# Two batches begin the rotary layers beside the last two batches' experts

## Chip, cores and metric

One core of a Trainium2 chip runs the whole program. The metric is the device time in microseconds (us); the three timed runs of the kernel before gave 4245.79, 4249.10 and 4255.25 us, so their median is 4249.1 us. Engine names are those of the profile: PE (TensorE), DVE (VectorE), ACT (ScalarE), POOL (GpSimd), SP (SyncE, whose queue issues all transfers).

## What is computed

The input x has 4 batches of 512 tokens with 128 features. The reference adds eight blocks in turn, each on a layer norm of x:

```python
x = x + L0_xcond(...)   # 3 rounds of slot attention against 77 context rows      -> stage 0
x = x + L0_ffn(...)     # 8 experts, top 2 of the 7 farthest, by similarity       -> stage 1
x = x + L1_xcond(...)   # 16 heads of 64, keys: 512 tokens and 77 context rows    -> stage 2
x = x + L1_ffn(...)     # 8 experts, the best one                                 -> stage 3
x = x + L2_xcond(...)   # self attention, cross attention, gated feed forward     -> stage 4
x = x + L2_ffn(...)     # 16 experts of width 64 in 4 groups, and shared ones     -> stage 5
x = x + L3_xcond(...)   # 6 layers, 16 heads of 8 with rotary positions           -> stage 6
x = x + L3_ffn(...)     # feed forward on the better half of the tokens           -> stage 7
```

One of the 6 rotary layers is: normalise, scale and shift; queries and keys projected and rotated by position; softmax(q k / sqrt 8) v over 512 tokens with a mask; the same again against the 77 context rows; a feed forward layer of width 512. Stages 6 and 7 are planned together, so "stage 6" below means both.

## The kernel before

**How the order comes about.** The kernel is a planner and five engine programs. Each piece of work is a Python generator that yields a `Want`: a chain of engines with estimated costs, and the buffers that it takes. `Plan.merge` always takes the Want whose key is smallest (the estimated time at which its first engine can begin, terms for work done and for the kind of chain, and a seeded random term), advances the planner's clocks and lets the generator emit its steps. The resulting list is the order of the instructions on every engine; each engine then runs strictly in its own order and waits on semaphores. The constants of the key are set for each stage in `ORDER`.

**Streams.** In stage 0 four streams run, one for each batch. After it, `fence("0")` closes the list of stage 0 and the clocks are levelled. Then two chains run (c.i is 0 and 1); chain 0 takes batches 0 and 2, chain 1 batches 1 and 3, through stages 1 to 5. In the expert stages 1, 3 and 5 `ahead` lets the gates of the second batch be computed beside the experts of the first. When both chains are through stage 4, the weights of rotary layers 0 and 1 are loaded into the two slots `WL` of the area wA (`lay0`), and `init6` is spawned: POOL fills the query and key areas of the four batches (memsets, L2706 and L2710) and SP then writes the mask rows into them (L1386 to L1391). When both chains are through stage 5, `bar` makes PE, ACT, DVE and POOL wait for each other, `mk6` (DVE) writes the mask columns of the value tiles, and the four streams `stage6` begin with `context6`, which projects the context's keys and values for each layer.

**A rotary layer** (`layer`): `ln6` (statistics L2156 and L2160 on DVE, the power on POOL, the normalisation L2169 on DVE or L2717 on POOL, transposes L1779, ACT L2061); `rope` twice, for keys and queries: PE projects (L1788, four matmuls in two banks), DVE multiplies by cosine and sine (L2538), POOL adds the halves and splits the sum into three bf16 parts (L2723 to L2736), and SP copies the parts to the tiles KS and QS (L1400). The value projection is L1796. Then `attn6`. Its softmax subtracts an exact row maximum, so `maxima` comes ahead of the scores: for self attention 32 reductions in each batch (`m8`: two matmuls at L1815, one reduction at L2549), for cross attention 8 (`m8c`: L1827, L2556). After each half of them `m8t` splits the maxima into a high and a low bf16 part (DVE L2562, L2564), PE transposes them (L1837), ACT copies the result (L2081), and SP writes it (`md`, L1405) into two rows of the query tile. Then `s8` makes the scores (L1847), ACT the exponential (L2088), and `a8` multiplies by the values (L1861).

**Tiles that matter here.** In stage 5 the second batch of a chain keeps its small tiles at columns 4096 to 4904 of its area `ar`, where the value tile V8 of batches 0 and 1 lies in stage 6. The experts' step in stage 5 is L1750 (two projections, four matmuls), L1756 (the weight spread over the rows), DVE L2506 and L2511, and L1764 (back to 128 features); DVE L2516 and L2518 add the result to X. In stages 0 and 1 the lines are L2249 (DVE, result of stage 0 to X), L1469 and L1538 (transposes and gates) and L1572 and L1580 (experts).

## Time and profile before

| what | value |
|---|---|
| median of three runs | 4249.1 us |
| the profiled execution, own time | 4243.65 us |
| its span, first to last instruction | 4241.9 us |
| mean granted TensorE clock | 0.956 |
| PE busy | 3750.9 us (88%) |
| DVE busy | 2500.4 us (59%) |
| ACT busy | 2365.3 us (56%) |
| POOL busy | 1356.9 us (32%) |

Busy shares are means over the span, and the stages have different limits: the tables by stretch say what an engine did in one stage. In a row of the timeline, the number in square brackets is the time the engine stood idle before the instruction, and what ended it. A granted clock of 1.00 is 2.4 GHz and 0.50 is 1.2 GHz.

### The profile page before, as it was taken

What the parts mean: (1) busy time and instruction counts of PE and PEld (TensorE: products, weight loads), DVE (VectorE), ACT (ScalarE), POOL (GpSimd) and SP (SyncE); (2) the same over time, 40 slices, a digit from 0 to 9 for tenths busy, and PEclk for the clock granted to TensorE, in tenths of its full rate; (3) what the DMA queues carried; (4) which work ended last, traced back from release to release, by engine and by line L of the source; (5) the groups of instructions that cost most, each with busy time, mean ns of one, the idle gap of its engine ahead of it and who ended that gap; (6) DMA issues with size and microseconds to landing.
All of it is one profiled execution on the core that took longest, in us unless ns stands there. A gap on an engine that the chain in (4) does not pass through costs nothing.

```text
span 4241.9 us, 58462 instructions
## 1 busy us (share of the span) xinstructions
PE 3750.9 (88%) x23161; PEld 1690.0 (40%) x23161; DVE 2500.4 (59%) x4892; ACT 2365.3 (56%) x3312; POOL 1356.9 (32%) x1333
## 2 busy tenths in 40 slices
PE   5599999899999998998886789988899898898996
PEld 3377433333774334334453123333333333332333
DVE  6731444544224444543566977787777777777754
ACT  4543554454335545555421477676676777767783
POOL 5500233334003430351033133434434343342412
PEclk8699999999999999999987899999999999999997
DMA  2000100000000001001101110210201101111100
GB/s 96 20 1 1 40 16 21 11 11 21 26 1 34 17 26 37 6 21 45 31 28 43 27 32 24 59 29 24 64 24 36 52 27 44 42 39 31 40 12 16
DMA packets 103826, 124.73 MB, mean 29 GB/s; under 512 B 25059, under 2 KB 88747, under 8 KB 101624
## 3 DMA queue, kind: packets, MB, share of 16 engines
q1 hardware_dynamic: 103552, 120.99, 9.5%
q8 instruction: 182, 2.98, 0.3%
q14 instruction: 92, 0.75, 0.1%
HBM read 58.00 MB, written 1.45 MB: 14 GB/s over the span
## 4 chain that ended last, share of the span: by engine, by line
PE 60%; DVE 23%; ACT 7%; POOL 6%; issue 2%; DMA 1%; SPq 0%; POOLq 0%; DVEq 0%; ACTq 0%
PE ps L1676 6%; PE ps L1660 6%; PE ps L1580 6%; PE ps L1572 5%; PE ps L1861 5%; DVE c1sm L2549 4%; DVE c0sm L2549 4%; PE ps L1788 3%; PE ps L1847 2%; PE ps L1708 2%; PE ps L1601 2%; PE ps L1815 2%; ACT wB L2088 2%; PE ps L1905 2%; POOL c1m L2717 2%
## 5 line engine op out<-in xcount | busy, mean ns | idle before, releaser
L2088 ACT ACTIVATE wB<-ps 128x1024 f32<-128x1024 f32 (+1 forms) x771 | 771.9, 1022 | 252.3 <-PE ps L1847 244.8
L2549 DVE TENSOR_REDUCE c1sm<-ps 128x2 f32<-128x1024 f32 x384 | 454.2, 1218 | 107.5 <-PE ps L1815 105.2
L2549 DVE TENSOR_REDUCE c0sm<-ps 128x2 f32<-128x1024 f32 x384 | 452.0, 1218 | 95.7 <-PE ps L1815 94.3
L2386 DVE TENSOR_REDUCE c1sm<-ps 128x2 f32<-128x1024 f32 x128 | 151.2, 1218 | 182.5 <-PE ps L1625 181.8
L2386 DVE TENSOR_REDUCE c0sm<-ps 128x2 f32<-128x1024 f32 x128 | 151.9, 1219 | 174.8 <-PE ps L1625 174.3
L2088 ACT ACTIVATE c0m<-ps 128x1024 f32<-128x1024 f32 (+1 forms) x189 | 193.2, 1022 | 59.0 <-PE ps L1847 57.4
L1861 PE MATMUL ps<-wB,c1m 128*9 128x512 f32 (+1 forms) x1224 | 202.2, 601 | 0.2 <-ACT wB L2088 0.2
L1660 PE MATMUL ps<-c0ar 64*128 64x512 f32 (+1 forms) x640 | 176.8, 629 | 13.6 <-DVE c1sm L2386 5.9
L1847 PE MATMUL ps<-c0ar 64*128 64x512 bf16 (+1 forms) x864 | 164.5, 386 | 26.8 <-DVE c1sm L2549 8.2
L2656 POOL TENSOR_SCALAR c0ve<-c0mv 128x4 f32<-128x4 f32 x25 | 6.2, 249 | 561.5 <-DVE c0mv L2160 550.3
L1660 PE MATMUL ps<-c1ar 64*128 64x512 f32 (+1 forms) x640 | 178.5, 634 | 8.0 <-ACT c1ar L2015 4.6
L1847 PE MATMUL ps<-c1ar 64*128 64x512 bf16 (+1 forms) x864 | 165.1, 390 | 21.9 <-DVE c0sm L2549 7.2
L2656 POOL TENSOR_SCALAR c0sm<-c0sm 128x4 f32<-128x4 f32 x40 | 7.8, 195 | 531.9 <-DVE c0sm L2160 453.5
L2700 POOL TENSOR_TENSOR c0ar<-c0ar 128x1024 f32<-128x1024 f32 x52 | 123.5, 2374 | 170.0 <-ACT c0ar L2022 137.3
L1815 PE MATMUL ps<-c0ar 62*128 62x512 bf16 x768 | 152.3, 397 | 25.1 <-DVE c0sm L2549 12.1
L2723 POOL TENSOR_TENSOR c0m<-c0m 128x512 f32<-128x512 f32 (+1 forms) x78 | 96.1, 1234 | 239.7 <-DVE c0m L2538 217.8
L2022 ACT ACTIVATE c1ar<-ps 128x1024 f32<-128x1024 f32 (+1 forms) x97 | 99.3, 1024 | 128.0 <-PE ps L1663 126.8
L1815 PE MATMUL ps<-c1ar 62*128 62x512 bf16 x768 | 151.5, 395 | 21.2 <-DVE c1sm L2549 7.4
L2656 POOL TENSOR_SCALAR c1sm<-c1sm 128x4 f32<-128x4 f32 x40 | 7.8, 195 | 500.4 <-DVE c1sm L2160 499.4
L2022 ACT ACTIVATE c0ar<-ps 128x1024 f32<-128x1024 f32 (+1 forms) x96 | 98.3, 1024 | 115.3 <-PE ps L1663 113.3
L2700 POOL TENSOR_TENSOR c1ar<-c1ar 128x1024 f32<-128x1024 f32 x53 | 126.1, 2379 | 113.1 <-ACT c1ar L2022 84.8
L1580 PEld LDWEIGHTS ps<-wA,c0m 128*128 128x128 f32 x1024 | 134.1, 193 | 56.9 <-issue 56.4
(841 smaller groups left out, 8609.2 us busy)
## 6 DMA issues: line engine op xcount, KB each, us to landing
c0ar<-c0m SPq DMA_DIRECT2D x216, 128.0 KB, 2.4
c1ar<-c0m SPq DMA_DIRECT2D x216, 128.0 KB, 2.4
c0m<-rscr SPq DMA_DIRECT2D x96, 128.0 KB, 2.9
c1m<-rscr SPq DMA_DIRECT2D x96, 128.0 KB, 2.9
wA<-in_lay SPq DMA_DIRECT2D x6, 1346.0 KB, 5.8
wA<-in_w SPq DMA_DIRECT2D x1, 4248.0 KB, 21.9
wA<-in_w SPq DMA_DIRECT2D x1, 4104.0 KB, 13.7
wA<-in_w4b SPq DMA_DIRECT2D x1, 2948.0 KB, 9.6
```

What stands on the lines that cost most here:

```text
L1572: e.matmul(u.ap, w1, z, start=True, stop=True).then_inc(*T(("ex1", n), free=[zt] if zt else []))
L1580: i = e.matmul(j4(acc.ap, j), j4(h.ap, j), w2, start=(k == 0 and j == 0), stop=(k == 3), skip_group_check=True)
L1660: e.matmul(j4(u.ap, h, 512)[0:n, :], c.KT[s][r, o:o + n], c.QT[s][r, :], start=True, stop=False)
L1676: x = e.matmul(acc.ap[64 - 64 * h:128 - 64 * h, :], c.VV[g % 2][0:n, i, 64 * h:64 * h + 64], P.ap[0:n, h, :], start=first, stop=end, skip_ ...
L1815: i = e.matmul(j4(u.ap, p, 512), c.QS[r, s, 128 * j:128 * j + 128], c.KS[r, s, :], start=True, stop=True)
L1847: i = e.matmul(j4(u.ap, p, 512)[0:n, :], K, c.QS[r, s, :], start=True, stop=True)
L1861: x = e.matmul(acc.ap[32 * i:32 * i + (9 if g % 2 else 18), :], vv, Ps[i // 2].ap[0:n, i % 2, :], start=first, stop=end, skip_group_check= ...
L2022: e.activation(P.ap[0:n, :, :], u.ap[0:n, :].rearrange("p (h q) -> p h q", h=2), ACT.Exp, scale=0.125).then_inc(*A(("P", n0, g, i), free=[u]))
L2088: e.activation(P.ap[0:n, :, :], u.ap[0:n, :].rearrange("p (a q) -> p a q", a=2), ACT.Exp, scale=S8).then_inc(*A(("P8", n0, s, k), free=[u]))
L2386: e.tensor_reduce(c.sm[:, 2 * (g % 2), 2 * j:2 * j + 2], u.ap.rearrange("p (h k) -> p h k", h=2)[:, :, 0:n], AX, ALU.max, negate=True).the ...
L2549: e.tensor_reduce(c.mneg[:, s // 4, j, :, s % 4], u.ap.rearrange("p (a k) -> p a k", a=2), AX, ALU.max, negate=True).then_inc(*V(free=[u]))
L2700: e.tensor_tensor(S.ap, P0.ap if P0 else S.ap, P.ap, ALU.add).then_inc(*G(("S", n0, g), free=[P0, P] if P0 else [P]))
```

## The change

Three things are done, and the planner's constants of stages 5 and 6 are set anew (stage 5: `held` 0.05 to 0.0066, `table` 2.0 to 2.1037, `spread` 1.0 to 1.0158, seed 2625 to 1721, three of the biases; stage 6 in the diff).

- **Stage 0 is joined to stage 1.** Instead of two merges with a fence and levelled clocks between them, one merge runs from the start to the end. A chain begins stage 1 when its own first batch is through stage 0; its second batch's gates wait until that batch is through (`zero`). When all four batches and the adaptive scales are through, fence 0, the load of w2 and `init64` are emitted (`through`), and the constants of stage 1 come in. The steps of stage 0 are planned by the same constants and seed as before.
- **Batches 0 and 1 begin stage 6 early.** After the experts of its first batch a chain spawns `begin6`. It waits in the planner for the last step of `init6`, marks all engines (`fence(("h", i))`), lets DVE wait for those marks (`hs`), and runs `stage6` for that batch: layer norm, projections, rotation and all 32 reductions. Values, the transposed maxima and the scores come only when `opened` is set, behind the bar of stage 5. Until then the two batches work in the slot of layer 1's weights (`E6` for the transposed activations, and `ER`, one buffer of 1280 columns, for the normalised activations and for every rotation of both batches), and their running sum `y` lies behind that slot. So layer 1's weights are loaded later, by `lay1`, whose transfer waits on SP for the early rotations and the two value projections. Batches 2 and 3 and `context6` begin behind the bar.
- **Cross attention's maxima are turned once.** `m8w` and `mw` treat all eight slices together (one split on DVE, four transposes of 32 rows on PE, one copy on ACT, two transfers) where `m8t` and `md` ran twice. Self attention keeps two halves. The tiles mneg and MS are laid out for both.

```diff
--- before.py
+++ after.py
...
-    "6": dict(lag=0.0689, weight=0.0152, even=0.002, held=0.2395, table=1.1712, apart=56.5442, spread=0, seed=9094, stagger=13.3148, bias=dict(T=0.244, S=0.373, VTA=-0.191, TVb=-0.054, A=-0.534, VG=-0.949, G=-0.490, TA=-0.046, TAb=-0.043)),
+    "6": dict(lag=0.0241, weight=0.0152, even=0.002, held=0.2549, table=1.1712, apart=56.5442, spread=0, seed=3843, stagger=13.3148, bias=dict(T=0.244, S=0.373, VTA=-0.191, TVb=-0.054, A=-0.534, VG=-0.949, G=-1.010, TA=-0.046, TAb=-0.043)),
...
-            e.mneg = s[:, 64:128].rearrange("p (h j a s) -> p h j a s", h=2, j=4, a=2)
-            e.MS = s[:, 128:192].bitcast(BF).rearrange("p (h j r) -> p h j r", h=2, j=4)
+            e.mneg = s[:, 64:128].rearrange("p (j a h s) -> p j a h s", j=4, a=2, h=2)
+            e.MS = s[:, 128:192].bitcast(BF).rearrange("p (j h r) -> p h j r", j=4, h=2)
+            e.MW = s[:, 128:192].bitcast(BF).rearrange("p (j r) -> p j r", j=4)
...
-            e.y = carve(512).rearrange("p (t d) -> p t d", t=4)
+            e.y = wA[:, 2 * LCOLS + 512 * e.i:2 * LCOLS + 512 * e.i + 512] if e.i < 2 else carve(512)
+            e.y = e.y.rearrange("p (t d) -> p t d", t=4)
...
+        E6 = Bufs([wA[:, LCOLS + 512 * k:LCOLS + 512 * k + 512] for k in range(2)])
+        ER = Bufs([wA[:, LCOLS + 1024:LCOLS + 2304]])
...
-        def ahead(gates, rest, c):
+        def ahead(gates, rest, c, then=None):
 
             q, got = c.alt, []
             q.ring = c.ring
 
             def second():
+                while 2 + c.i not in zero:
+                    yield
                 got.append((yield from gates(q, 2 + c.i, 0.0)))
 
             g = yield from gates(c, c.i, 0.0)
             plan.spawn(second(), c)
             yield from rest(c, c.i, *g)
+            if then:
+                plan.spawn(then(c), six[c.i])
             while not got:
                 yield
             yield from rest(q, 2 + c.i, *got[0])
 
-        begun, done, quarter = {}, {}, []
+        begun, done, quarter, zero, opened = {}, {}, [], set(), []
+
+        def through(what):
+
+            zero.add(what)
+            if len(zero) == 5:
+                fence("0")
+                emit("load", "w2", "wB", "0")
+                plan.stage("1")
+                for c in cos:
+                    plan.spawn(init64(c), c)
+
+        def scales():
+            yield from adaptive()
+            through("ada")
+
+        def opening(c):
+
+            yield from stage0(c, c.i)
+            through(c.i)
+            if c.i < 2:
+                while "en" not in first:
+                    yield
+                c.work = ORDER["0"]["stagger"] + ORDER["1"]["apart"] * c.i
+                yield from chain(c)
 
         def chain(c):
 
             for name, run in (("1", lambda: ahead(stage1, experts1, c)), ("2", lambda: both(stage2, c)),
                               ("3", lambda: ahead(stage3, experts3, c)), ("4", lambda: both(stage4, c)),
-                              ("5", lambda: ahead(stage5, experts5, c))):
+                              ("5", lambda: ahead(stage5, experts5, c, begin6))):
+                while name == "2" and len(zero) < 5:
+                    yield
                 if name in "24":
                     pairs_of_ring(c)
                 elif name in "35":
                     ring_of_pairs(c)
                 if name not in begun:
                     begun[name] = c
-                    plan.stage(name)
+                    if name != "1":
+                        plan.stage(name)
                     emit("gate", {"1": ("w_w1", "w1"), "2": ("w_w2", "w2"), "3": ("w_w3", "w3"), "4": ("w_w4a", "w4a"),
                                   "5": ("w_w5", "w5")}[name])
                 yield from run()
                         emit("load", "w4b", "wA", "3")
                         emit("sel")
                     elif name == "4":
-                        for l in range(2):
-                            emit("lay0", l)
+                        emit("lay0", 0)
                         plan.spawn(init6())
+                    elif name == "5":
+                        emit("bar", "5")
+                        plan.level(banks)
+                        emit("mk6")
+                        plan.stage("6", six)
+                        opened.append(True)
+                        for e in six[2:]:
+                            plan.spawn(stage6(e), e)
+                        plan.spawn(context6())
+
+        def begin6(c):
+
+            e = six[c.i]
+            e.work = c.work
+            while "i6" not in first:
+                yield
+            fence(("h", c.i))
+            emit("hs", c.i)
+            yield from stage6(e)
...
+            first["i6"] = True
...
             def maxima():
-                for h in range(2):
+                if cross:
+                    for s in range(8):
+                        (u,), t = yield Want([("T", .27), ("V", .73)], [two], tq, True)
+                        emit("m8c", c, l, n0, s, qn, kkeys, u)
+                        two.give(u, t[1])
+                    (u,), t = yield Want([("V", .5), ("T", .35), ("A", .6)], [banks], t[1])
+                    emit("m8w", c, n0, u)
+                    banks.give(u, t[2])
+                    _, t = yield Want([("S", 1.3)], after=t[2])
+                    emit("mw", c, n0)
+                    got[0] = got[1] = t[0]
+                    return
+                def half(h):
+                    t = (0.0, tq)
                     for s in range(4 * h, 4 * h + 4):
-                        if cross:
-                            (u,), t = yield Want([("T", .27), ("V", .73)], [two], tq, True)
-                            emit("m8c", c, l, n0, s, qn, kkeys, u)
+                        for j in range(4):
+                            (u,), t = yield Want([("T", .32), ("V", 1.24)], [two], tq, True)
+                            emit("m8", c, n0, s, j, qn, kkeys, u)
                             two.give(u, t[1])
-                        else:
-                            for j in range(4):
-                                (u,), t = yield Want([("T", .32), ("V", 1.24)], [two], tq, True)
-                                emit("m8", c, n0, s, j, qn, kkeys, u)
-                                two.give(u, t[1])
-                    (u,), t = yield Want([("V", .42), ("T", .35), ("A", .6)], [banks], t[1])
+                    return t[1]
+
+                def turned(h, t):
+                    (u,), t = yield Want([("V", .42), ("T", .35), ("A", .6)], [banks], t)
                     emit("m8t", c, n0, h, u)
                     banks.give(u, t[2])
                     _, t = yield Want([("S", 1.3)], after=t[2])
                     emit("md", c, n0, h)
                     got[h] = t[0]
+
+                if opened:
+                    for h in range(2):
+                        t = yield from half(h)
+                        yield from turned(h, t)
+                    return
+                for h in range(2):
+                    t = yield from half(h)
+                while not opened:
+                    yield
+                for h in range(2):
+                    yield from turned(h, t)
 
...
-        lay_ready = {0: True, 1: True}
+        lay_ready = {0: True}
+        early = []
         lay_done = {}
         kc = {}
         cross_done = {}
             b = c.i
             w = WL[l % 2]
             s, sh = ada(3 + 3 * l, b)
-            zt, key, t = yield from ln6(c, c.t, s, sh, "G" if l else "V")
+            begins = l == 0 and b < 2
+            zb, ztb, rb = (ER, E6, ER) if begins else (G6, G6, R6)
+            zt, key, t = yield from ln6(c, c.t, s, sh, "G" if l else "V", zb, ztb)
             got = {}
 
             def keys():
-                got["k"] = yield from rope(f"k{b}", w["k"], zt.ap, key, 512, c.KS, KR, [c.ks_free], t)
+                got["k"] = yield from rope(f"k{b}", w["k"], zt.ap, key, 512, c.KS, KR, [c.ks_free], t, rb)
 
             def queries():
-                got["q"] = yield from rope(f"q{b}", w["q"], zt.ap, key, 512, c.QS, QR, [c.qs_free], t)
+                got["q"] = yield from rope(f"q{b}", w["q"], zt.ap, key, 512, c.QS, QR, [c.qs_free], t, rb)
+
+            n = uid()
+
+            def values():
+                while not opened:
+                    yield
+                (u,), tv = yield Want([("T", 1.1), ("A", 1.15)], [banks], t)
+                emit("v8", c, n, w["v"], zt, key, u, c.vf)
+                banks.give(u, tv[1])
+                got["v"] = tv[1]
+
+            def over():
+                while len(got) < 3:
+                    yield
+                emit("endz", zt)
+                ztb.give(zt, max(got["v"], t))
+                if begins:
+                    early.append((b, got["k"][0], got["q"][0], n))
+                    if len(early) == 2:
+                        yield from do("lay1", list(early), chain=[("S", .7)], after=got["v"])
+                        lay_ready[1] = plan.clock["S"] + 30.0
 
             plan.spawn(keys(), c)
             plan.spawn(queries(), c)
-            n = uid()
-            (u,), tv = yield Want([("T", 1.1), ("A", 1.15)], [banks], t)
-            emit("v8", c, n, w["v"], zt, key, u, c.vf)
-            banks.give(u, tv[1])
+            plan.spawn(values(), c)
+            plan.spawn(over(), c)
...
-        plan.stage("0", four)
-        plan.merge([context(), constants()] + [stage0(c, c.i) for c in four] + [adaptive(), norms()], [None, None] + four)
-        fence("0")
-        plan.level(banks)
-        emit("load", "w2", "wB", "0")
-        for c in cos:
-            c.work = ORDER["1"]["apart"] * c.i
-        plan.merge([chain(c) for c in cos] + [init64(c) for c in cos], cos)
-        emit("bar", "5")
-        plan.level(banks)
-        emit("mk6")
-        plan.stage("6", six)
-        plan.merge([stage6(c) for c in six] + [context6()], six)
+        plan.stage("0")
+        for c in four:
+            c.work = ORDER["0"]["apart"] * (c.i // 2)
+        plan.merge([context(), constants()] + [opening(c) for c in four] + [scales(), norms()], [None, None] + four)
         fence("6")
...
+            def lay1(uses):
+                for b, kn, qn, vn in uses:
+                    w.wait_ge(*D(f"k{b}").at(("rp", kn)))
+                    w.wait_ge(*D(f"q{b}").at(("rp", qn)))
+                    w.wait_ge(*T.at(("v8", vn)))
+                e.dma_start(wA[:, LCOLS:2 * LCOLS], d["lay"][1]).then_inc(*D("w_l1")(("lay", 1)))
...
+            def mw(c, n0):
+                w.wait_ge(*A.at(("mT", n0)))
+                for p in range(2):
+                    e.dma_start(c.QS[64 * p + 62:64 * p + 64, :, :], c.mT[16 * p:16 * p + 16, :]
+                                ).then_inc(*D(f"m{c.i}_0")(("m", n0, 0)))
...
+            def hs(i):
+                for q in (T, A, V, G):
+                    w.wait_ge(*q.at(("f", ("h", i))))
...
+            def m8w(c, n0, u):
+                MW = c.MW.rearrange("p j (a x h s) -> p (j a) x (h s)", a=2, x=2, h=2)
+                hi, lo, m = MW[:, :, 0, :], MW[:, :, 1, :], c.mneg.rearrange("p j a h s -> p (j a) (h s)")
+                w.wait_ge(*V.now())
+                e.tensor_copy(hi, m).then_inc(*V())
+                w.wait_ge(*V.now())
+                e.tensor_tensor(lo, m, hi, ALU.subtract).then_inc(*V(("ms", n0)))
+                mss[c.i, 0] = mss[c.i, 1] = V.n
```

## Rows read from the trace of the kernel before

**Rows 1.** The page, chain of waits that ended last, by engine.

```profile
PE 60%; DVE 23%; ACT 7%; POOL 6%; issue 2%; DMA 1%; SPq 0%; POOLq 0%; DVEq 0%; ACTq 0%
```

**Rows 2.** By stretch: PE, PEld, DVE, ACT, POOL busy (count), PE clock, DMA share, GB/s.

```profile
190.00:210.00 20.00, 2.97 (x12) 2.49 (x12) 13.13 (x59) 3.73 (x7) 5.75 (x12) 0.50 0.29 106
2190.00:2212.00 22.00, 20.24 (x94) 12.61 (x92) 14.33 (x49) 3.44 (x5) 0.67 (x1) 1.00 0.03 8
2212.00:2263.50 51.50, 50.27 (x214) 30.93 (x214) 22.44 (x33) 9.54 (x14) 0.00 (x0) 0.97 0.00 1
2263.50:2320.00 56.50, 28.64 (x86) 17.01 (x86) 37.93 (x120) 8.05 (x23) 29.35 (x40) 0.67 0.22 57
2320.00:2377.00 57.00, 28.56 (x98) 5.87 (x97) 56.67 (x53) 0.00 (x0) 15.40 (x16) 0.58 0.16 43
2390.00:4050.00 1660.00, 1489.22 (x10983) 534.97 (x10981) 1285.83 (x1993) 1187.50 (x1400) 620.93 (x739) 0.99 0.13 37
...
2900.00:3000.00 100.00, 85.97 (x652) 29.15 (x650) 77.98 (x116) 69.20 (x81) 34.49 (x40) 0.98 0.15 42
```

**Rows 3.** Timeline of DVE about the end of stage 5.

```profile
2145.32 0.69 DVE L2516 TENSOR_TENSOR X<-X,ps 128x512 f32<-128x512 f32 x1
...
2230.90 0.69 DVE L2516 TENSOR_TENSOR X<-X,ps 128x512 f32<-128x512 f32 x1 [2.33 <-PE ps L1770]
...
2262.75 0.69 DVE L2516 TENSOR_TENSOR X<-X,ps 128x512 f32<-128x512 f32 x1 [2.33 <-PE ps L1770]
...
2266.82 0.87 DVE L2156 BATCH_NORM_STATS2 c0sm<-X 128x6 f32<-128x128 f32 x4
...
2358.22 18.18 DVE L2549 TENSOR_REDUCE c0sm<-ps 128x2 f32<-128x1024 f32 x16
2376.43 0.18 DVE L2562 CAST c0sm<-c0sm 128x32 bf16<-128x32 f32 x1
```

**Rows 4.** Timeline of PE about the same place.

```profile
2257.74 1.88 PE L1750 MATMUL ps<-c1ar,wB 128*128 128x512 f32 x4
...
2285.70 1.88 PE L1788 MATMUL ps<-c1m,wA 128*128 128x512 f32 x4
...
2371.93 0.61 PE L1815 MATMUL ps<-c0ar 62*128 62x512 bf16 x2 [0.52 <-DVE c0sm L2549]
...
2382.34 0.39 PE L1815 MATMUL ps<-c0ar 62*128 62x512 bf16 x2
2382.57 0.38 PE L1847 MATMUL ps<-c0ar 64*128 64x512 bf16 x2
```

**Rows 5.** Timeline of POOL: memsets of init6, and one rotation's first and last step.

```profile
2137.96 7.11 POOL L2706 MEMSET c0ar<- 128x4096 bf16 x2
...
2188.52 2.15 POOL L2710 MEMSET c1ar<- 128x2464 bf16 x1
...
2334.62 1.26 POOL L2723 TENSOR_TENSOR c0m<-c0m 128x512 f32<-128x512 f32 x1 [2.54 <-DVE c0m L2538]
...
2338.54 1.15 POOL L2736 TENSOR_TENSOR c0m<-c0m 128x512 bf16<-128x512 f32 x1
```

**Rows 6.** Timeline of SP's queue: the first transfers of turned maxima.

```profile
2378.14 1.42 SPq L1405 DMA_DIRECT2D c0ar<-c0m  x2
```

**Rows 7.** Timeline of DVE: the same four normalisations beside a memset and without one.

```profile
2137.85 7.36 DVE L2169 TENSOR_SCALAR c1m<-X,c1mv,c1rs 128x128 f32<-128x128 f32 x4 [0.77 <-POOL c1rs L2658]
...
2377.64 1.11 DVE L2169 TENSOR_SCALAR c1m<-c1m,c1sm 128x128 f32<-128x128 f32 x4
```

**Rows 8.** Waits between 2390 and 4050: engine, line, whom; us in total, times, longest.

```profile
PE ps L1837 <- DVE c0sm L2564: 27.9, 42, 1.4
PE ps L1837 <- DVE c1sm L2564: 24.1, 36, 2.3
```

**Rows 9.** Timeline of PE: one batch's turn; stage 1's first expert matmuls.

```profile
2907.11 0.39 PE L1837 MATMUL ps<-IDB,c0sm 128*16 128x128 bf16 x4 [0.61 <-DVE c0sm L2564]
...
215.96 4.86 PE L1572 MATMUL ps<-c0m,wA 128*128 128x512 f32 x6
```

**Rows 10.** Timeline of DVE: the last result of stage 0 goes to X.

```profile
194.90 0.69 DVE L2249 TENSOR_TENSOR X<-X,c1ar 128x512 f32<-128x512 f32 x1
```

72 lines of the change are left out of this document (43 added, 29 removed).

## Prediction, made before the changed kernel ran

> **What bounds the kernel now.** I read the chain of waits first: 60% of it is PE and 23% DVE [rows 1], so most of the time is worth what PE's time is worth, and a quarter of it is a DVE story. The busy time by stretch shows where. In the body of stage 6 PE is busy 1489.22 of 1660 us, 89.7%, beside DVE's 77.5% and ACT's 71.5% [rows 2]. The last 51.5 us of stage 5 are PE alone (50.27 us, DVE 22.44, POOL nothing) [rows 2]. Between them lies a hole: from 2263.5 to 2377 PE is busy 57.2 of 113.5 us at a granted clock of 0.67 and 0.58, and in its second half DVE is busy 56.67 of 57 us [rows 2]. The DVE timeline names the work: layer norms from 2266.82, then back to back reductions until 2376.43 [rows 3]; the PE timeline shows each pair of maxima matmuls waiting 0.52 us for the reduction before it, and the first score matmul at 2382.57 [rows 4]. Batch 0 had its result of stage 5 at 2145.32 and batch 1 at 2230.90; the last batch came at 2262.75 [rows 3]. A smaller hole lies between stages 0 and 1: in 190 to 210 PE is busy 2.97 of 20 us at 0.50 [rows 2].
>
> **Part 1, early batches.** When can they begin? Batch 0 is done at 2145.32 but must wait for the memsets, which end at 2190.67 [rows 5]. From the first layer norm to the end of the second projection took 20.8 us (2266.82 to 2287.58) [rows 3, 4]; a rotation takes POOL 5.1 us (2334.62 to 2339.69) [rows 5]. Keys and queries now share one buffer ER, so the second rotation waits for the first's transfers; I put 40 us from the start to the first reduction, against about 54 us before with four batches mixed (2266.82 to 2320, from where DVE does nothing but reduce) [rows 2, 3]. So batch 0 reduces from about 2230 and batch 1 from about 2275.
>
> What it adds to stage 5: PE gets two rotations' projections of 1.88 us each per batch and 32 pairs of 0.39 us [rows 4]: 3.8 + 12.5, with transposes some 17 us for batch 0 and 5 for what batch 1 reaches. PE is full there, so this is paid: stage 5 ends at 2263.4 + 22.5 = 2286. DVE is free 56% of it (22.44 of 51.5 busy) [rows 2]: from 2230 to 2286 that is 31 us, less 7 for batch 1's norms and rotation; a reduction takes 1.136 us (18.18 / 16) [rows 3], so about 21 of batch 0's 32 fit and 11 (12.5 us) are left.
>
> Behind the bar: mk6 about 2.5 us (between the last write to X and 2266.82) [rows 3], the 11 reductions 12.5, split, transposes and copy 1.7 (2376.43 to 2378.14) and the transfer with its landing 4.4 (2378.14 to 2382.57) [rows 3, 4, 6]. That is 21 us, and scores begin at 2307 instead of 2382.57: 75.5 us sooner. But less is done by then. Before, 48 reductions were done at 2377 and four batches normalised; now it is 32, two batches and one or two rotations fewer. PE is missing 16 x 0.39 + 3 x 1.88 + transposes = 13 us, which leaves 62. DVE is missing 16 x 1.136 + two batches' norms and three rotations, together about 31 us, which leaves 44. PE is the busier engine in stage 6, but DVE is close behind and nearly full at that start, so I take the middle, **53 us** (bounds 44 and 62).
>
> Waits that are added: `hs` makes DVE wait for PE twice, and the experts' multiplications queue behind it. Nearest row: one experts' step is 3.5 us (18 of them in 62 us), so 0 to 7 us, taken 3. `lay1` sits in SP's queue until both value projections are done, and behind it wait the transfers of the maxima and the rotations of batches 2 and 3; those projections are the first thing PE does behind the bar, so 0 to 5, taken 2. Layer 1's weights themselves are wanted a layer, some 300 us, later: nothing. POOL's rotation in stage 5 stands in an empty queue [rows 2]: nothing for POOL itself. Buffer ER holds only the early batches up: in the 40 us. The transfers (12 a batch for rotations) are the ones that SP issued behind the bar before.
>
> What POOL does to DVE shows in one pair of rows: four normalisations take 1.11 us alone and 7.36 us beside a memset of 7.11 us [rows 7]. The Trainium skill (SBUF — State Buffer, Who interferes with whom) says that the two engines share a port pair under an exclusive lock and the second comer waits for the whole instruction, while a reduction never contends; by that rule the early rotations (4 of 5.1 us) delay norms and gate chains in stage 5 and leave the reductions alone. The pair of rows agrees with the lock; the reductions' immunity no row here shows. From the rows alone, two early norms stretched as in rows 7 cost 2 x 6.2 = 12.5 us of DVE; it enters the rival below.
>
> **Part 2, stage 0 joined to 1.** The plan of stage 0 is the same up to the first batch's end. The last result is written at 194.90 [rows 10], and the first expert matmuls run at 215.96 [rows 9], 21 us later: norms, gates, a chain of small DVE instructions. If a batch is through some 10 us sooner, which no row here shows, it can have this chain beside the others' last steps, though on a DVE that is busy 13 of 20 us [rows 2]. Bounds 0 and 21; I take **10 us**.
>
> **Part 3, cross maxima once.** There are 24 cross attentions, each with one turn fewer. A turn costs PE 0.39 us of transposes, and in the row before it PE stood 0.61 us for DVE's split [rows 9]; over the body of stage 6 such waits are 52.0 us in 78 turns, 0.67 each [rows 8]. PE would save 24 x 1.06 = 25 us. Against it: the first scores of a cross attention now wait for all 8 reductions, four more; with four batches in flight other work covers that, with one left it is paid. And where DVE is the limit, a wait saved on PE only moves. Bounds 0 and 25, taken **13 us**.
>
> **The end.** Batches 0 and 1 now lead 2 and 3 by more, so at the end fewer run side by side. Nearest row: at the mixed share of 0.90 against a stretch with one or two batches I take 5 us (0 to 27, the latter if 80 us run at 60% where 90% was possible; both shares are estimates).
>
> **Sum.** 53 - 3 - 2 + 10 + 13 - 5 = 66 us. The profiled execution took 4243.65 us, 5.45 below the median; its own time after would be 4177.7, and a median beside 4249.1 comes to **4183 us**. A measurement of this kernel tells apart about 0.2%, 8.5 us.
>
> A rule that could shift the sum: that PE is "89.7% busy" need not mean that it is the limit. PE's weight loads are busy only 534.97 of 1660 us, 32% [rows 2]. The Trainium skill (Perfetto Trace Analysis, Identifying the Most-Contended Engine) calls matmul busy time a poor measure and wants weight-load share and FLOPs instead. By that, the limit in stage 6 would be DVE's chain, part 1 would be worth 44 and part 3 next to nothing: 44 us in all, 4205. By the rows, which show PE idle only in gaps of half a microsecond, it would be 62 and 25: 87 us, 4162. The middle stands; both ends go into the range.
>
> **Rivals.**
> - *Stage 5 becomes DVE's.* For it: DVE and PE queues are in order, and every experts' step passes through two DVE instructions; one reduction ahead of them in each of 18 steps costs up to 18 x 1.136 = 20 us, and the norms beside POOL 12.5. Against it: a step leaves DVE 2 of its 3.5 us free. The gain shrinks from 66 to 34: 4215.
> - *More than summed.* PE's account holds (62), stage 0's whole gap goes (21), all of part 3 (25) and no costs: 108 us, 4141.
> - *It doesn't do what it says.* The early batch is planned only once `init6`'s last step is, and if that comes late in stage 5's order, the early work lands at the bar. Then part 1 is worth little, and some 23 us remain: 4226. Against it: in the trace the memsets are over at 2190.67, 72 us before the stage ends [rows 5].
> - *Slower: stage 6's new order is looser.* All of stage 6 is planned anew with other constants and from another start, in five queues that are strictly in order. The place is its 1850 us; the price is PE's share: the worst slice has 85.97 of 100 where the mean is 89.7 [rows 2], and a whole stage at that share takes 1850 x (89.7 / 85.97 - 1) = 80 us more, 4263. It decides from a share under 86.6%. Against it: the old order's mean is three points above that.
>
> **Chances.** The forecast 0.58 (its own range 4160 to 4205), stage 5 on DVE 0.16, more than summed 0.12, not as it says 0.07, looser order 0.07. Between 4138 and 4217 lie the first three, less a little of each: 0.8. Faster by over 0.2% in the first three and nearly all of the fourth: 0.91; the same 0.03; slower 0.06.
>
> **What the profile would show.** Right if: reductions (L2549) stand between experts' steps from about 2230; the first score matmul (L1847) comes within 45 us of the last L2516, where it was 120; the clock in that stretch stays near 1.0; the stretch from there to the end is no longer than 1860 us; stage 1's experts begin by about 206; L1837 counts 288 where it was 384. Wrong if: DVE is full and PE under 90% busy in stage 5's second half; the early batches' first reductions come behind the bar; or stage 6's share of PE in whole slices lies at 87% or lower.

## The result, and the profile after

| | before | after |
|---|---|---|
| median | 4246.16 us (6 runs, 4240.75 to 4255.25) | 4267.51 us (6 runs, 4259.94 to 4282.97) |
| ratio, 95% interval | | 1.0053 [1.0041, 1.0066] |
| profiled execution, own time and span | 4243.65, 4241.9 us | 4259.94, 4258.0 us |

The changed kernel is slower by 0.5%, 21 us, where the forecast had it faster by 66 us.

The profile's page after, busy time and the chain of waits by engine. Against [rows 1] the chain is the same mixture; nothing in it names a new limit.

```profile
PE 3758.3 (88%) x23065; PEld 1691.6 (40%) x23065; DVE 2496.8 (59%) x4844; ACT 2364.1 (56%) x3297; POOL 1356.5 (32%) x1333
PE 61%; DVE 22%; ACT 7%; POOL 6%; issue 2%; DMA 1%; SPq 0%; POOLq 0%; DVEq 0%; ACTq 0%
```

Busy time by stretch of the changed kernel, for [rows 2]; the stretches follow its own landmarks: the end of stage 5 (2212 to 2266), the hole up to the first score (2266 to 2336), the body of stage 6 (2400 to 4060).

```profile
core 0: us, PE busy (x) PEld busy (x) DVE busy (x) ACT busy (x) POOL busy (x), PEclk, DMA share, GB/s
190.00:210.00 20.00, 11.76 (x36) 7.42 (x37) 12.51 (x59) 5.69 (x8) 4.73 (x10) 0.53 0.00 0
2212.00:2266.00 54.00, 53.39 (x222) 32.73 (x222) 33.43 (x75) 10.11 (x15) 9.70 (x12) 0.97 0.06 15
2266.00:2336.00 70.00, 36.10 (x131) 15.28 (x130) 58.80 (x109) 7.64 (x21) 22.17 (x29) 0.61 0.16 41
2400.00:4060.00 1660.00, 1465.57 (x10606) 526.95 (x10604) 1238.80 (x1901) 1142.96 (x1343) 622.31 (x741) 0.98 0.13 37
```

Stage 0's hole has more work in it (11.76 us of PE where it was 2.97), and the hole behind stage 5 is 70 us long where it was 120. But in the body of stage 6 PE is busy 1465.57 us where it was 1489.22. From the first score to the end it is 1921 us (2336.6 to 4258.0), where it was 1859 (2382.6 to 4241.9): the first score comes 46 us sooner, and 62 us are lost behind it.

The DVE timeline after, from batch 0's first layer norm of stage 6 to batch 1's first reductions, and the end of stage 5 between them (L2661 multiplies by cosine and sine in a rotation, L2672 is a reduction, L2639 the last experts' sum).

```profile
2225.78 0.87 DVE L2279 BATCH_NORM_STATS2 c0sm<-X 128x6 f32<-128x128 f32 x4 [0.20 <-PE ps L1868]
...
2248.56 1.22 DVE L2661 TENSOR_TENSOR wA<-ps,CST 128x1024 f32<-128x1024 f32 x1 [1.03 <-PE ps L1892]
2249.70 3.45 DVE L2292 TENSOR_SCALAR wA<-X,c1sm 128x128 f32<-128x128 f32 x4
...
2263.29 1.23 DVE L2661 TENSOR_TENSOR wA<-ps,CST 128x1024 f32<-128x1024 f32 x1 [0.97 <-PE ps L1892]
...
2266.16 0.69 DVE L2639 TENSOR_TENSOR X<-X,ps 128x512 f32<-128x512 f32 x1 [0.32 <-PE ps L1874]
...
2289.89 1.22 DVE L2672 TENSOR_REDUCE c0sm<-ps 128x2 f32<-128x1024 f32 x1
...
2292.15 8.01 DVE L2672 TENSOR_REDUCE c0sm<-ps 128x2 f32<-128x1024 f32 x7
...
2336.68 1.23 DVE L2661 TENSOR_TENSOR wA<-ps,CST 128x1024 f32<-128x1024 f32 x1 [1.75 <-PE ps L1892]
...
2362.87 8.00 DVE L2672 TENSOR_REDUCE c1sm<-ps 128x2 f32<-128x1024 f32 x7
```

Batch 0 begins 35 us later than I had it (2225.78 for 2191). Of these 35, 6 come from the memsets, which end at 2196.47 where they ended at 2190.67; the other 29 are the place that the planner gave the early batch in DVE's queue, since DVE stood idle only 0.20 us before that norm (its wait for `hs`). Its second rotation follows at 2263.29, 15 us behind the first (both use the one buffer ER), and meets the masks and batch 2's norms; not one reduction stands before the bar. Batch 1's rotations come at 2336.68 and 2352.25, 88 us behind batch 0's. The POOL timeline between the two norms of batch 0 and its second rotation shows that rotation cut up by the other work behind the bar:

```profile
2194.32 2.15 POOL L2843 MEMSET c1ar<- 128x2464 bf16 x1
2227.16 0.19 POOL L2789 TENSOR_SCALAR c0sm<-c0sm 128x4 f32<-128x4 f32 x1 [30.68 <-DVE c0sm L2283]
...
2264.59 1.26 POOL L2856 TENSOR_TENSOR wA<-wA 128x512 f32<-128x512 f32 x1 [9.61 <-DVE wA L2661]
...
2279.56 1.15 POOL L2869 TENSOR_TENSOR wA<-wA 128x512 bf16<-128x512 f32 x1
```

The PE timeline in the hole: as in [rows 4] each pair of maxima matmuls waits for the reduction before it, and each pair takes 0.61 us where it took 0.39 in [rows 4] (the granted clock from 2290 to 2330 was 0.56, so PE was mostly at the lower level); the last row is the first score.

```profile
2295.68 0.61 PE L1919 MATMUL ps<-c0ar 62*128 62x512 bf16 x2 [0.52 <-DVE c0sm L2672]
2296.82 0.61 PE L1919 MATMUL ps<-c0ar 62*128 62x512 bf16 x2 [0.52 <-DVE c0sm L2672]
...
2336.57 0.39 PE L1961 MATMUL ps<-c0ar 64*128 64x512 bf16 x2
```

The waits of PE in 2400 to 4060 for the split maxima: L1941 is the turn of self attention, L1950 the new one of cross attention. They answer to the 52.0 us of [rows 8] and come to 39.4.

```profile
PE ps L1941 <- DVE c1sm L2688: 18.3, 20, 1.5
PE ps L1941 <- DVE c0sm L2688: 11.5, 13, 1.4
...
PE ps L1950 <- DVE c1sm L2697: 5.2, 7, 1.5
PE ps L1950 <- DVE c0sm L2697: 4.4, 8, 1.0
```

### The profile page after: what moved, and what is told of

It reads as the page before. It is cut to its first block, busy times and chain, and to the rows that moved or that the text cites. A ratio compares the mean times of both kernels' runs of the same rounds, so it can differ in the third digit from the quotient of the medians.

```text
span 4258.0 us, 58144 instructions
## 1 busy us (share of the span) xinstructions
PE 3758.3 (88%) x23065; PEld 1691.6 (40%) x23065; DVE 2496.8 (59%) x4844; ACT 2364.1 (56%) x3297; POOL 1356.5 (32%) x1333
## 4 chain that ended last, share of the span: by engine, by line
PE 61%; DVE 22%; ACT 7%; POOL 6%; issue 2%; DMA 1%; SPq 0%; POOLq 0%; DVEq 0%; ACTq 0%
PE ps L1780 6%; PE ps L1764 6%; PE ps L1684 6%; PE ps L1676 5%; PE ps L1975 5%; DVE c1sm L2672 4%; DVE c0sm L2672 4%; PE ps L1892 3%; ACT wB L2207 3%; PE ps L1961 2%; PE ps L1919 2%; PE ps L1705 2%; PE ps L2011 2%; PE ps L1812 2%; PE ps L2019 2%
## 5 line engine op out<-in xcount | busy, mean ns | idle before, releaser
L2672 DVE TENSOR_REDUCE c1sm<-ps 128x2 f32<-128x1024 f32 x384 | 457.5, 1220 | 109.8 <-PE ps L1919 106.8
L2672 DVE TENSOR_REDUCE c0sm<-ps 128x2 f32<-128x1024 f32 x384 | 456.9, 1219 | 76.2 <-PE ps L1919 72.7
L1975 PE MATMUL ps<-wB,c1m 128*18 128x512 f32 (+1 forms) x1232 | 204.4, 608 | 1.6 <-ACT wB L2207 1.4
L1919 PE MATMUL ps<-c0ar 62*128 62x512 bf16 x768 | 155.4, 404 | 29.1 <-DVE c0sm L2672 17.3
L1684 PEld LDWEIGHTS ps<-wA,c1m 128*128 128x128 f32 x1024 | 131.5, 192 | 50.6 <-issue 50.0
```

What stands on the lines that cost most here:

```text
L1684: i = e.matmul(j4(acc.ap, j), j4(h.ap, j), w2, start=(k == 0 and j == 0), stop=(k == 3), skip_group_check=True)
L1919: i = e.matmul(j4(u.ap, p, 512), c.QS[r, s, 128 * j:128 * j + 128], c.KS[r, s, :], start=True, stop=True)
L1975: x = e.matmul(acc.ap[32 * i:32 * i + (9 if g % 2 else 18), :], vv, Ps[i // 2].ap[0:n, i % 2, :], start=first, stop=end, skip_group_check= ...
L2672: e.tensor_reduce(c.mneg[:, j, :, s // 4, s % 4], u.ap.rearrange("p (a k) -> p a k", a=2), AX, ALU.max, negate=True).then_inc(*V(free=[u]))
```

## The experiments

Times are medians, each beside runs of the kernel before on the same chip (its medians were 4243.0 to 4246.2); ratios are to that. "Scores to end", "round" and "spread" are from the one profiled execution, whose time can lie up to 9 us from the median (the changed kernel's 7.6 below it, that of x_after_count 8.8 above). A **round** is a quarter of the time between batch 3's end of layer 0 and its end of layer 4; the **spread** is the time from batch 0's to batch 3's end of the same layer, over layers 1 to 4. The ends of layers are read as follows: the last instruction of a layer for a batch is the sum behind the second matmul of its feed-forward block, and its instances stand in the queue in the order batch 0, 1, 2, 3 (in x_after_old56 batch 0 ends a layer before batch 3 has ended the one before it; there the tiles tell them apart). Kernel before, DVE timeline: the four ends of layer 0, the leader's end of layer 1, and batch 3's end of layer 4:

```profile
2508.49 0.69 DVE L2586 TENSOR_TENSOR c0m<-c0m,ps 128x512 f32<-128x512 f32 x1 [1.62 <-PE ps L1905]
2583.38 0.69 DVE L2586 TENSOR_TENSOR c1m<-c1m,ps 128x512 f32<-128x512 f32 x1 [2.54 <-PE ps L1905]
2661.30 0.69 DVE L2586 TENSOR_TENSOR c1m<-c1m,ps 128x512 f32<-128x512 f32 x1 [2.35 <-PE ps L1905]
2726.70 0.69 DVE L2586 TENSOR_TENSOR c1m<-c1m,ps 128x512 f32<-128x512 f32 x1 [3.84 <-PE ps L1905]
2806.71 0.69 DVE L2586 TENSOR_TENSOR c0m<-c0m,ps 128x512 f32<-128x512 f32 x1 [2.54 <-PE ps L1905]
...
3943.62 0.69 DVE L2586 TENSOR_TENSOR c1m<-c1m,ps 128x512 f32<-128x512 f32 x1 [2.54 <-PE ps L1905]
```

The same in the changed kernel:

```profile
2490.70 0.69 DVE L2719 TENSOR_TENSOR wA<-wA,ps 128x512 f32<-128x512 f32 x1 [2.54 <-PE ps L2019]
2565.05 0.69 DVE L2719 TENSOR_TENSOR wA<-wA,ps 128x512 f32<-128x512 f32 x1 [1.74 <-PE ps L2019]
2648.97 0.69 DVE L2719 TENSOR_TENSOR c0m<-c0m,ps 128x512 f32<-128x512 f32 x1 [2.75 <-PE ps L2019]
2720.45 0.69 DVE L2719 TENSOR_TENSOR c1m<-c1m,ps 128x512 f32<-128x512 f32 x1 [3.23 <-PE ps L2019]
2763.00 0.69 DVE L2719 TENSOR_TENSOR wA<-wA,ps 128x512 f32<-128x512 f32 x1 [8.32 <-PE ps L2019]
...
3983.88 0.69 DVE L2719 TENSOR_TENSOR c1m<-c1m,ps 128x512 f32<-128x512 f32 x1 [2.75 <-PE ps L2019]
```

Here lies the first part of the answer. Before, the batches are 65 to 80 us apart and go round evenly. After, batch 0 ends layer 0 18 us sooner, batch 3 only 6; batch 0 then takes 272 us for layer 1 where it took 298, and stays ahead. The same rows split the span. Batch 3 is through layer 0 6.3 us sooner; its next four layers take 1263.4 us where they took 1216.9, 46.5 more; and from there to the end it is 274.1 us where it was 298.2, 24.1 less, the other batches being further on by then. Together that is the 16.1 us between the two profiled executions (4258.0 and 4241.9). So four times the difference of two rounds overstates the loss when the spreads differ.

| kernel | us | ratio [95%] | scores to end | round | spread |
|---|---|---|---|---|---|
| before | 4246 | | 1859 | 304 | 222 to 228 |
| after | 4267.5 | 1.0053 [1.0041, 1.0066] | 1921 | 316 | 267 to 282 |
| x_join | 4239.0 | 0.9985 [0.9975, 0.9994] | 1867 | 306 | 224 to 231 |
| x_cross | 4252.3 | 1.0012 [1.0000, 1.0025] | 1868 | 304 | 223 to 234 |
| x_nocross | 4308.5 | 1.0141 [1.0122, 1.0160] | 1972 | 320 | 268 to 280 |
| x_noearly | 4260.5 | 1.0034 [1.0021, 1.0046] | 1879 | 305 | 228 to 235 |
| x_noearly_old56 | 4236.2 | 0.9978 [0.9968, 0.9987] | 1855 | 302 | 219 to 232 |
| x_after_old56 | 4405.1 | 1.0377 [1.0362, 1.0393] | 2081 | 336 | 374 to 384 |
| x_pert_before | 4292.1 | 1.0112 [1.0097, 1.0127] | 1913 | 311 | 234 to 239 |
| x_pert_after | 4300.4 | 1.0119 [1.0094, 1.0144] | 1965 | 323 | 273 to 279 |
| x_noearly_lag | 4244.5 | 1.0000 [0.9991, 1.0009] | 1864 | 301 | 223 to 231 |
| x_noearly_held | 4265.5 | 1.0051 [1.0031, 1.0070] | 1889 | 304 | 224 to 242 |
| x_after_held | 4283.9 | 1.0089 [1.0071, 1.0106] | 1944 | 320 | 276 to 279 |
| x_noearly_old_lag | 4248.4 | 1.0008 [0.9999, 1.0018] | 1871 | 306 | 224 to 242 |
| x_after_hold | 4338.1 | 1.0227 [1.0210, 1.0244] | 1993 | 325 | 272 to 284 |
| x_after_lag_hold | 4330.4 | 1.0199 [1.0184, 1.0215] | 1989 | 325 | 268 to 280 |
| x_noearly_hold | 4256.9 | 1.0034 [1.0021, 1.0047] | 1880 | 302 | 219 to 232 |
| x_before_hold | 4324.2 | 1.0187 [1.0172, 1.0203] | 1930 | 308 | 232 to 239 |
| x_after_count | 4257.2 | 1.0025 [1.0015, 1.0035] | 1917 | 307 | 224 to 238 |
| x_after_old56_count | 4224.4 | 0.9952 [0.9939, 0.9966] | 1894 | 303 | 223 to 235 |

### The parts one by one

In these expectations theory L is a loss from the uneven start that the early batches give stage 6, C a loss from the single turn of the cross maxima, P that any new order of stage 6 scatters the time.

x_cross, the kernel before with part 3 alone (in `attn6`):

```diff
             def maxima():
+                if cross:
+                    for s in range(8):
...
+                    emit("m8w", c, n0, u)
...
+                    emit("mw", c, n0)
+                    got[0] = got[1] = t[0]
+                    return
```

> The kernel before with cross attention's maxima turned once, nothing else; planner constants as before. Theory L (the loss of the changed kernel comes from the early batches: stage 6 from a lopsided start): the single turn is worth what the prediction said, so this is 5 to 20 us faster than before. Theory C (the loss comes from the single turn, because scores now wait for all eight cross reductions, and only this makes the body of stage 6 looser): this is 15 to 40 us slower than before. Theory P (any new order of stage 6 scatters the time, whatever is changed): anything within 25 us either way, with PE's share of the body of stage 6 the only thing that moves.

x_join, the kernel before with part 2 alone (`opening`, `through`, `scales` and one merge):

> The kernel before with stage 0 joined to stage 1, nothing else. In the changed kernel everything up to the end of stage 3 ran 11.2 us earlier (last expert sum of stage 3 at 1304.1 for 1315.3). Theories L and C: this kernel is 8 to 14 us faster than before, as the gain is carried through to the end. Theory P: 11 us are there at the end of stage 3, but chain and batch phases enter the later stages shifted, and the end differs by up to 25 us more or less.

x_nocross, the changed kernel with the cross maxima turned twice, as before:

> The changed kernel with cross attention's maxima turned in two halves again; early batches, joined stages and new constants stay. Theory L: no faster than the changed kernel (4267), rather 5 to 20 us slower. Theory C: 25 to 50 us faster than the changed kernel, so clearly faster than before. Theory P: within 25 us of the changed kernel, either way.

x_noearly, the changed kernel without early batches, with its own constants:

```diff
-                              ("5", lambda: ahead(stage5, experts5, c, begin6))):
+                              ("5", lambda: ahead(stage5, experts5, c))):
...
-                        for e in six[2:]:
+                        for e in six:
...
-            begins = l == 0 and b < 2
+            begins = False
```

The rest of its edit follows from this: layer 1's weights are loaded with layer 0's again, and behind the bar all four batches are staggered by their number, as in the kernel before.

> The changed kernel without the early batches: all four begin stage 6 behind the bar, both layers' weights are loaded at the end of stage 4; joined stages, single cross turn and new constants stay. Theory L: the loss is gone, 4215 to 4240 us, the 11 us of the join and what the single turn is worth below before; PE's share in the body of stage 6 back at 89.7%. Theory C: still slower than before, and slower than the changed kernel by the 46 us of head start that its first scores had: 4270 to 4310. Theory P: no forecast beyond the head start, 4240 to 4310.

Part 2 does what was summed: stages 3 to 5 end 8 to 10 us sooner (stage 5 at 2253 for 2263), and the median is 7 us lower. Part 3 is +7 us by itself (an interval that begins at no difference, 1.0000) and -41 us inside the changed kernel, with the same operations saved, each in a single order: a difference of that kind isn't the price of an operation. The early batches cost 7 us where 53 - 3 - 2 - 5 = 43 were summed for them. Parts 2 and 3 together, with the change's constants, come to 4260.5 where their single effects add to 4245.6. Neither L nor C holds as it was put: x_cross is neither 5 to 20 us faster nor 15 to 40 slower, and x_nocross lost 41 us, more than any of the three allowed; P's wide ranges hold the other three.

### Constants, and the scatter of orders

Theory K, in the next two: the new constants cost the time. x_after_old56 is the changed kernel with both constant lines taken from before; x_noearly_old56 has them too, and no early batches.

```diff
-    "5": dict(lag=0.3, weight=0.0424, even=0, held=0.0066, table=2.1037, apart=0, spread=1.0158, seed=1721, bias=dict(G=1.346, TVA=-0.769, TAV=0.401, S=0.791, VG=-1.033, TVb=-0.255, TV=0.185, T=1.188, V=-1.043)),
-    "6": dict(lag=0.0241, weight=0.0152, even=0.002, held=0.2549, table=1.1712, apart=56.5442, spread=0, seed=3843, stagger=13.3148, bias=dict(T=0.244, S=0.373, VTA=-0.191, TVb=-0.054, A=-0.534, VG=-0.949, G=-1.010, TA=-0.046, TAb=-0.043)),
+    "5": dict(lag=0.3, weight=0.0424, even=0, held=0.05, table=2.0, apart=0, spread=1.0, seed=2625, bias=dict(G=0.872, TVA=-0.769, TAV=0.748, S=0.791, VG=-1.033, TVb=-0.255, TV=0.185, T=1.359, V=-1.043)),
+    "6": dict(lag=0.0689, weight=0.0152, even=0.002, held=0.2395, table=1.1712, apart=56.5442, spread=0, seed=9094, stagger=13.3148, bias=dict(T=0.244, S=0.373, VTA=-0.191, TVb=-0.054, A=-0.534, VG=-0.949, G=-0.490, TA=-0.046, TAb=-0.043)),
```

> The changed kernel with the planner's constants of stages 5 and 6 from the kernel before (lag, held, table, spread, seed, three biases); all three parts of the change stay. Theory L (the loss is the uneven start that the early batches give stage 6, whatever the constants): the stretch from the first score matmul to the end stays near 1921 us, and the time within 10 us of 4267. Theory K (the new constants cost the time, by the delay of chain 1 in stages 4 and 5 or a bad order of stage 6): the stretch falls to some 1885 and the time to some 4230. Theory P (any new order of stage 6 scatters the time by tens of us): anything from 4240 to 4300, with no relation to the constants' origin.

> The changed kernel without its early batches and with the constants of stages 5 and 6 from the kernel before: only the joined first stages and the cross maxima turned once are left. If their measured effects add (4239.0 and 4252.3 against 4245.7), 4245.5 us. Theory K: near that, 4240 to 4250, some 15 us under the 4260.5 of the same kernel with the new constants. Theory L: the constants are no part of the loss, so the 4260.5 stays within 5 us. Theory P: 4235 to 4275.

x_pert_before and x_pert_after move `lag` of stage 6 by 0.011 and nothing else:

> The kernel before with one of the planner's numbers for stage 6 moved a little (lag 0.0689 to 0.0800), which alters the order of the five queues in stage 6 and nothing else: no operation is added or taken away. Theory P: the time moves by 10 us or more, to 4255 to 4290, and PE's share in the body of stage 6 from 89.6% to under 89%. Theories L and K: the order's details are worth little, and the time stays within 5 us of 4245.7.

> The changed kernel with the same step of the same number (lag 0.0241 to 0.0350): again only the order in stage 6 differs. Theory P: the time moves by 10 us or more in either direction from 4267.5 (4250 to 4290). Theory L: it stays within 5 us, since the uneven start is the same.

One number of the planner, moved a little, costs 46 us in the kernel before and 33 in the changed one, with every operation the same. L's forecast for that (within 5 us) fell. P had the size right (10 us or more), though both times lie just above its ranges (4292.1 for at most 4290, 4300.4 for at most 4290), and PE's share of the body in x_pert_before is 89.3%, not under 89; x_after_old56 lies beyond all theories, and x_noearly_old56 4 us under K's range. Without the early batches the constants of before bring 24 us; with them they cost 138. Four more kernels follow; three of them complete two more pairs with and without the early batches, and the last shows the kernel of the old constants, without early batches, in a second order:

> The changed kernel without its early batches, at the same nearby order number as the earlier perturbation (lag 0.0350). With the early batches that number gave 4300.4; without them and at the change's own number it was 4260.5. Theory P (each order has its own scatter, and the early batches themselves are worth little): between 4250 and 4290, the early batches' worth at this number anywhere from -50 to +10. Theory L (the early batches cost by their uneven start at every order): at least 7 us under 4300.4 in each of the pairs of this call, so 4293 or less here.

> The changed kernel without its early batches, another number of stage 6's planner moved a little (held 0.2549 to 0.2600). Theory P: 4245 to 4290, not the 4260.5 of the same operations at the change's number. Theory L: under its partner with early batches by 7 us or more.

> The changed kernel with held 0.2549 to 0.2600 in stage 6, all three parts in place. Theory P: since the change's own number was presumably picked for its time, a neighbour is slower: 4275 to 4310. Theory L: over its partner without early batches by 7 us or more.

> Joined first stages and cross maxima once, the constants of the kernel before but lag 0.0689 to 0.0800, the step that cost the kernel before 46 us (4245.9 to 4292.1). Theory P: it costs here as well, though not the same: 4250 to 4300, and not 4236.2. If the two small parts are worth 10 us at any order, the mean of this and 4236.2 lies 10 us under the mean of the kernel before at its two numbers, 4269.0: 4282 here.

The first and the last came out just below P's ranges. The pairs, with and without the early batches: 4267.5 and 4260.5, 4300.4 and 4244.5, 4283.9 and 4265.5, 4405.1 and 4236.2. The early batches cost 7, 56, 18 and 169 us: in all four pairs, as L wanted, though the size goes with the order. The table shows what is common: with them a spread of 267 us or more and a round of 316 or more, without them at most 242 and 311. In the worst of them the leader runs into the next layer's weights, whose load waits for the last batch to end the layer two before. Waits of x_after_old56 from 2350 on; none of this kind is in the kernel before or after.

```profile
PEld ps L1961 <- DMA wA<-in_lay: 18.6, 3, 6.3
PE ps L1961 <- DMA wA<-in_lay: 17.9, 3, 6.1
DVE c1sm L2279 <- DMA wA<-in_lay: 17.0, 3, 5.7
```

### Holding the leader back

If the head start of 46 us made the spread, a pause for batch 0 should mend it (theory S; U says that the early batches cost something of their own). The same edit in four kernels:

```diff
                 emit("gate", (f"w_l{l}", ("lay", l)))
+                if c.i == 0 and l == 1:
+                    c.t += 40.0
                 yield from layer(c, l)
```

> The changed kernel; in the planner batch 0 may begin layer 1 only 40 us after its layer 0 ended (nothing else changed). Theory S: the spread from batch 0 to batch 3 at the end of layers 1 to 4 falls from 270 to 282 us to 225 to 245, the round from 315 to about 304, and the time by 15 to 40 us from 4267.5, to 4225 to 4252, though work was held back. Rival U: no gain, 4260 to 4300.

> The changed kernel at lag 0.0350 (4300.4 without the delay) with the same delay of batch 0. Theory S: under 4275, spread 225 to 250. Rival U: 4290 to 4310.

> The fastest kernel so far (joined first stages and cross maxima once, no early batches, constants of the kernel before, 4236.2) with the same delay of batch 0 at the start of layer 1. Its batches are evenly spaced already (75 to 80 us), so by theory S the delay spoils that (spread about 185 to 200, a gap of over 100 behind batch 3): 4250 to 4290, or the planner lets batch 0 catch up and it stays within 10 us. Rival U: within 10 us of 4236, scatter aside.

> The kernel before with the same delay of batch 0. Theory S: slower, 4255 to 4300, spread at layers 1 and 2 under 200. Rival U: within 10 us of 4246, scatter aside (the one step of lag measured 46 us).

Theory S fell in this form: the two early kernels lost 71 and 30 us. Without early batches the pause cost 21 us (4256.9 for 4236.2) and, in the kernel before, 78. But the spread told more than the time. It came back within a layer, to 267 to 284 us with early batches and to 219 to 239 without, whatever the pause. So something acts all through stage 6 and pulls to a set spread. (Against the expectation the spread of the kernel before didn't fall under 200 either. Its 78 us, at an even spread, are scatter or the pause itself; that is open.)

### The account of work

The planner picks the next step by the time at which it could begin, plus `even` (0.002) times the batch's `work`: a batch that has had less comes first. `stage("6", six)` sets the accounts to 56.5 times the batch number, which is what keeps the batches apart. The change calls it behind the bar, when batches 0 and 1 have already worked, so the early work drops out of the accounts. By the planner's own sums batch 0 stands at 201 at the end of its layer 0 where all its work is 226, 25 short, and batch 1 is 7 short; with the constants of before it is 83 and 51. These sums give the spread that is measured. One layer of a batch is 224 units (227 in the kernel before), and by the accounts batch 3 ends its layer 0 at 170 units more than batch 0 in the kernel before, 196 in the changed one and 253 in x_after_old56. If the planner keeps the accounts level, that is 170/227, 196/224 and 253/224 of a round of 304, 316 and 336 us: an estimate of 228, 276 and 379 us, where 222 to 228, 267 to 282 and 374 to 384 were measured. By theory W the reset makes the spread, and the spread costs the time; by its rival U the time stays. The edit counts the early work and does nothing else:

```diff
+                        done6 = [e.work - e.work0 for e in six[:2]]
                         plan.stage("6", six)
+                        for e, w0 in zip(six, done6):
+                            e.work += w0
...
-            e.work = c.work
+            e.work = e.work0 = c.work
```

> The changed kernel, with the early work of batches 0 and 1 added to their accounts when stage 6's accounts are set; no operation is added or taken away. Theory W: the spread at the ends of layers 1 to 4 falls from 267 to 282 us to 222 to 242, the round from 315 to about 304, and the time to 4205 to 4250 (head start of 46 us kept, scores to end 1865 to 1900 instead of 1921). Rival U: spread or not, the time stays at 4260 to 4300.

> The same account in the kernel with all three parts and the constants of stages 5 and 6 from before, which took 4405 us at a spread of 375 us. Theory W: spread 222 to 245, round 303 to 310, time 4205 to 4265, a fall of 140 us or more by an account of 82 and 51 units. Rival U: over 4330, since stage 5 still ends at 2308 us and the early batches are as early.

Both spreads fell to where those without early batches are (282 to at most 238, 384 to at most 235), and both rounds with them (316 to 307, 336 to 303). The times fell by 181 us and by 10; the 4257.2 us of the latter are above the range expected, and so are its 1917 us from the first score to the end. The split of the span shows where the rest of it went: in x_after_count batch 3's four layers take 34 us less than in the changed kernel (1229 for 1263), and the stretch behind them 38 us more (312 for 274). With the lead gone, more is left to do when batch 3 ends layer 4. (Its first score came 10 us later, 2346.4 for 2336.6, though the order of instructions up to the bar is the same in both; its stage 5 ended at 2276.0 for 2266.2 in these two executions.)

The second kernel takes **4224.4 us**, less than the kernel before (0.9952 [0.9939, 0.9966]), than the changed one, and than the same without early batches (4236.2). Its body of stage 6 beside that of x_after_old56, same columns as above, the first row x_after_old56:

```profile
2400.00:4060.00 1660.00, 1378.93 (x9852) 498.04 (x9856) 1136.02 (x1747) 1044.53 (x1242) 569.71 (x677) 0.94 0.12 34
```

```profile
2400.00:4060.00 1660.00, 1486.79 (x10874) 539.51 (x10871) 1265.30 (x1981) 1175.43 (x1387) 626.61 (x747) 0.99 0.13 37
```

PE does 1486.79 us of work in it for 1378.93, and at a clock of 0.99 for 0.94. With the account mended, the early batches are worth what is left of the pairs: 4257.2 against 4260.5, and 4224.4 against 4236.2: 3 and 12 us, one order each, so within what one number of the planner moves. The DVE timeline of x_after_old56_count (reductions L2675, experts' step L2632, last experts' sum L2642) shows one reason why not more:

```profile
2253.39 1.23 DVE L2675 TENSOR_REDUCE c0sm<-ps 128x2 f32<-128x1024 f32 x1 [0.53 <-PE ps L1922]
2255.30 0.75 DVE L2632 SCALAR_TENSOR_TENSOR c1m<-ps,wB,c1m 128x512 f32<-128x512 f32 x1 [0.68 <-PE ps L1857]
2256.98 6.88 DVE L2675 TENSOR_REDUCE c0sm<-ps 128x2 f32<-128x1024 f32 x6
2265.38 1.23 DVE L2664 TENSOR_TENSOR wA<-ps,CST 128x1024 f32<-128x1024 f32 x1 [1.52 <-PE ps L1895]
2266.52 12.53 DVE L2675 TENSOR_REDUCE c0sm<-ps 128x2 f32<-128x1024 f32 x11
...
2304.43 6.87 DVE L2675 TENSOR_REDUCE c1sm<-ps 128x2 f32<-128x1024 f32 x6
2312.03 0.69 DVE L2642 TENSOR_TENSOR X<-X,ps 128x512 f32<-128x512 f32 x1 [0.72 <-PE ps L1877]
```

One reduction stands beside the experts. The others stand in a row behind them and before the last sum, which came at 2259 without early batches and comes at 2312 here. The hole has only moved to the other side of the bar. Busy time in it, the same kernel, 2259 to 2312.5:

```profile
2259.00:2312.50 53.50, 32.49 (x102) 9.77 (x102) 49.65 (x45) 0.00 (x0) 9.57 (x10) 0.59 0.11 30
```

DVE 49.65 of 53.5 us, PE at a clock of 0.59: [rows 2] for 2320 to 2377, once more. Even so the first score comes 54 us sooner than in x_noearly_old56 (2323.9 for 2378.4) and batch 3 is through layer 0 31 us sooner (2697 for 2728); 12 us of that go in the stretch behind batch 3's layer 4 (310 for 298) and 3 in the rounds, which leaves the 15 us between the two profiled executions. Why that last stretch is longer is open.

## Why the prediction was wrong

**The sign.** The step that failed is the one in part 1 that turned "scores begin 75.5 us sooner" into "53 us" by the work that PE and DVE would be missing, and carried that unchanged to the end. It assumed a stage 6 that mixes as well as before. It did not: the scores began 46 us sooner, batch 3 was through layer 0 only 6 us sooner, and the four layers after that took 46.5 us more. The planner lost part of two batches' work from its accounts and let the leader run ahead, and on top of this every order of stage 6 has a scatter of tens of us that the sum had as a single rival with 0.07.

The ratios, set against 4246 us, take the result apart along one path: joined stages and single turn with the constants of before -9; the change's constants +24; the early batches with their work counted -4; their work not counted +12; together +23. Against the sum of -66 that is 89 us: 14 in parts 2 and 3 (23 summed, 9 measured), 39 in the early batches even with their work counted (43 summed, 4 measured), 24 in the constants, which the sum had at nothing without a reason, and 12 in the account. Each of these steps is one order against one order, and a step under some 40 us is not told apart from scatter by itself. Along another path, with the constants last, it is -9, -11, +181 and -138: the change's constants cost time except where they keep the fault small (25 units uncounted for 83). (That they bring a given sum is not to be read from single orders: without early batches their three orders took 4244.5 to 4265.5 us, the two of the old lines 4236.2 and 4248.4.)

**Start of the early batches.** Given as reductions from 2230 and 2275; they came at 2289.89 and 2362.87. The 40 us from start to first reduction were 64, since ER is one buffer and the second rotation fell behind the bar, and the start itself was 35 us late. With the old constants and the account mended they came at 2253.39, and 1 of the 21 that I put beside the experts stood there. The shares were read rightly (DVE is free half of the time), but 56% free in 51.5 us is no room for work that becomes ready at their end.

**Stage 5's end.** Given as 2286, 22.5 us of added work; it is 2266.2 in the changed kernel, with no reduction squeezed in, against 2262.5 in x_noearly: 4 us. It is 2312 where the reductions are. My rival of a stage 5 on DVE has its place right there, with 53 us for the 20 and 12.5 I gave it, but not its way: the reductions don't stand one by one ahead of the experts' steps, they stand in a row ahead of the last sum.

**First score.** Given as 2307, was 2336.57: a head start of 46 us, 29 less. As I read the rows, it came mostly from doing batch 0's maxima ahead of the others' (batch 1's began 73 us behind), which is a change of order and saves no work. What counted was when batch 3 was through layer 0: 2720 for 2727.

**`hs`, `lay1`, the lock.** `lay1` went out at 2361, a layer ahead of its use, and no wait for those weights shows: the 2 us were right or too much. `hs` made DVE idle for 0.20 us before batch 0's norm (2225.78) and not at all before batch 1's (2243.66), for the 3 us given.

**Part 2.** 10 us given, 7 measured in x_join, 10 at its end of stage 5: right. In the changed kernel itself 11 us are there at the end of stage 3 (1304.1 for 1315.3), and at the end of stage 5 it is 3 us late (2266.2 for 2262.8). 4 us of that are the early work; the rest isn't told apart between the constants of stage 5 and the differences of single executions. Its scene was right as well: stage 1's experts begin at 203.

**Part 3.** 13 us given. The transposes fell from 384 to 288 as said, and the waits on PE by 12.6 us (52.0 to 39.4), but neither goes with the time. Alone (x_cross) the same waits fell by 23 us, to 29.1, and the time rose by 7; inside the change they fell by 3, from 42.3 in x_nocross to 39.4, and the time fell by 41. The part's own worth stays open. A wait that leaves the list needn't leave the time when the order around it is another.

**The rule on busy PE.** With DVE's chain as the limit all came to 44 us, with PE's share to 87. Neither decided, since neither engine's amount of work did: with the same operations PE was busy 83% of the body in x_after_old56 and 90% in x_after_old56_count.

**The rivals.** The looser order was the one that came, at nearly its price (4263 for 4267.5), and that nearness is luck. Its point of decision, a share under 86.6%, was wrong: the share is 88.3%. The price was read from one slice's share, 80 us laid on a gain of 66. Measured, 46 us were gained up to the first score and 62 lost behind it: 40 up to batch 3's end of layer 0 (384 us for 344), 46.5 in its next four layers, less 24 in the last stretch. "It doesn't do what it says" (4226) came in part too: the early batch was planned late, and all its reductions landed behind the bar. My mark "no longer than 1860 us from the first score" was also wrong by my own sum, since a start with less done has more behind it (1859 + 75.5 - 53 - 13 + 5 = 1874); the 1921 were clear all the same. The marks that spoke rightly against me: the reductions behind the bar, the score later than 45 us behind stage 5, and the clock of 0.61 in the hole. Of those for it, only the start of stage 1's experts and the 288 transposes came.

**What stays open.** Why a wide spread costs some 4% of a round. In x_after_old56 a part is the wait for the layer weights; at 270 us there is no such wait, and the tested repair shows that spread and round go together, not by what. Why x_after_count gained only 10 us of the rounds' 34: the last stretch took the rest in the profiled executions, and how far the scatter of its one order hides more isn't shown. What the change's constants cost in the kernel before isn't known either: no run has it with them.

## What to carry to other kernels

The queues of this kernel are written by a greedy planner, and one of its numbers, moved a little, shifted the time by 5 to 46 us in six trials. In such a kernel a part must be judged in several neighbouring orders with and without it, never from one. A change that starts some streams early must carry over all the planner's state about them: here a line that resets an account was worth 10 to 181 us. And read an early start by when the last stream is through its first round, not by when the first one scores; and look at the last stretch too, since what a lead costs in the rounds comes back there in part.

## What the runs showed of the hardware

Four normalisations took 3.45 us at 2249.70 beside POOL's rotation in SBUF (1.11 alone [rows 7]), while 7 reductions from PSUM took 8.01 us, 1.14 each, at 2292.15 beside the next rotations on POOL, no more than while POOL did nothing (8.00 us at 2362.87). The POOL timeline after, at both places:

```profile
2249.86 1.30 POOL L2856 TENSOR_TENSOR wA<-wA 128x512 f32<-128x512 f32 x1 [3.55 <-DVE wA L2661]
...
2293.64 1.28 POOL L2863 CAST c0m<-c0m 128x512 bf16<-128x512 f32 x2
2295.00 1.15 POOL L2865 TENSOR_TENSOR c0m<-c0m 128x512 f32<-128x512 f32 x1
```

The prediction had left open whether reductions are immune, for want of a row. The Trainium skill (SBUF — State Buffer, Who interferes with whom) says that on this chip a reduction on DVE never contends with POOL; by that rule, the trace agrees.

The clock gives a loose order a second price. In the body of stage 6 the granted clock was 0.98 to 1.00 in the kernels with a spread up to 242 us, 0.96 to 0.98 in those with 267 to 284, and 0.94 in x_after_old56, where PE is busy least; the same 23065 matmuls were busy 3785.4 us in it over the whole span, 3758.3 in the changed kernel and 3743.8 in x_after_old56_count.
